# Two crossbar transposes of a tile each, joined into one transfer of two tiles, in a two-layer attention kernel

## The reference

```python
# first block                                   # second block
theta, phi = W_theta x + b, W_phi x + b         # h = group_norm(x1);  q, k, v = conv1x1(h)
f = softmax(theta^T phi / 8)                    # attn = softmax(q^T k * 128 ** -0.5)
x1 = x + W_fuse (f x) + b_fuse                  # y = x1 + W_p (attn v) + b_p
```

## Time and profile before

| | |
|---|---|
| median of 3 runs | 1957.88 us (1955.1 to 1966.29) |
| profiled execution | 1956.89 us, span 1955.1 us |
| PE busy | 1757.1 us, 90% |
| DVE busy | 1481.1 us, 76% |
| ACT busy | 1454.8 us, 74% |
| POOL busy | 1271.6 us, 65% |
| transposing transfers | 384, 4.5 us from issue to landing in the median |

### The profile page before, as it was taken

The page is one execution under the profiler, slowest core; times in us unless marked ns, Lnnn a source line. Parts: engine busy times, 40 slices in busy tenths (PEclk is TensorE's granted clock), DMA queues, the critical chain, the costliest instruction groups (busy, mean ns, idle before and its releaser), DMA issues.

```text
span 1955.1 us, 34447 instructions
## 1 busy us (share of the span) xinstructions
PE 1757.1 (90%) x8966; PEld 1202.4 (62%) x8966; DVE 1481.1 (76%) x1650; ACT 1454.8 (74%) x2152; POOL 1271.6 (65%) x1321
## 2 busy tenths in 40 slices
PE   5799999999999999999999999899999999989986
PEld 3566666666666666666666666666666666666654
DVE  4677777778777878777877777877777877787754
ACT  4577777777777777777777777777777777777764
POOL 2565776666776666776666776666676666776653
PEclk9899999999999999999999999999999999999999
DMA  3587787777777777787777778777778777767774
GB/s 76 113 152 140 150 160 153 148 153 149 150 160 153 152 146 149 149 162 154 145 152 149 151 160 157 143 149 149 152 152 162 145 149 150 151 148 155 144 133 92
DMA packets 860085, 286.33 MB, mean 146 GB/s; under 512 B 822304, under 2 KB 823200, under 8 KB 860064
## 3 DMA queue, kind: packets, MB, share of 16 engines
q1 hardware_dynamic: 860064, 286.08, 73.9%
HBM read 50.86 MB, written 17.04 MB: 35 GB/s over the span
## 4 chain that ended last, share of the span: by engine, by line
PE 47%; issue 22%; DVE 12%; POOL 9%; ACT 7%; DMA 1%; SPq 1%; DVEq 1%; POOLq 0%; ACTq 0%
PE o_ps L414 16%; PE s_ps L414 14%; PE m_ps L414 13%; PE s_ps L452 4%; ACT et L618 3%; POOL pair L837 2%; DVE phi L793 2%; DVE theta L789 2%; POOL y_sb L936 2%; DVE neg_max L700 2%; DVE x L754 2%; POOL h_lo L837 2%; ACT e_copied L608 2%; DVE den_scaled L729 1%; POOL rstd L877 1%
## 5 line engine op out<-in xcount | busy, mean ns | idle before, releaser
L414 PE MATMUL o_ps<-et,v_hi 128*128 128x512 f16 x2048 | 697.2, 382 | 89.0 <-DVE x L754 58.5
L700 DVE TENSOR_REDUCE neg_max<-s_ps 128x1 f32<-128x1024 f32 x512 | 625.6, 1222 | 127.1 <-PE s_ps L414 116.8
L414 PEld LDWEIGHTS o_ps<-et,v_hi 128*128 128x128 f16 x2048 | 202.4, 99 | 345.1 <-issue 163.6
L414 PE MATMUL o_ps<-et,v_lo 128*128 128x512 f16 x1024 | 389.5, 380 | 0.0
L608 ACT ACTIVATE s_ps<-s_ps,neg_max 128x1024 f32<-128x1024 f32 x256 | 278.3, 1087 | 111.4 <-DVE neg_max L700 110.5
L717 DVE SCALAR_TENSOR_TENSOR pair<-s_ps,pair 128x1024 f16<-128x1024 f32 x256 | 312.5, 1221 | 52.2 <-ACT pair L633 51.3
L414 PE MATMUL s_ps<-phi,theta 128*128 128x512 f32 x1024 | 331.9, 447 | 6.9 <-ACT e_copied L608 4.0
L711 DVE SCALAR_TENSOR_TENSOR et<-s_ps,et 128x1024 f16<-128x1024 f32 x128 | 156.7, 1225 | 219.7 <-ACT et L618 219.7
L837 POOL TENSOR_TENSOR pair<-e_copied,pair 128x1024 f16<-128x1024 f32 x128 | 274.3, 2143 | 16.5 <-ACT pair L631 16.5
L926 POOL TENSOR_TENSOR x<-x,xr 128x512 f32<-128x512 f32 x64 | 81.5, 1274 | 309.0 <-DVE x L754 309.0
L633 ACT ACTIVATE pair<-s_ps 128x1024 f16<-128x1024 f32 x256 | 261.9, 1023 | 8.1
(11 more groups left out here) (113 smaller groups left out, 3185.3 us busy)
## 6 DMA issues: line engine op xcount, KB each, us to landing
rden_row<-rden_dram SPq DMA_DIRECT2D x128, 256.0 KB, 3.8
xs<-in_x SPq DMA_DIRECT2D x32, 512.0 KB, 4.6
phi<-phi SPq DMA_DIRECT2D x64, 256.0 KB, 3.1
out_y<-y_sb SPq DMA_DIRECT2D x64, 256.0 KB, 2.7
et<-pair SPq DMA_TRANSPOSE x384, 4.5
rden_dram<-rden SPq DMA_DIRECT2D x128, 2.0 KB, 2.1
w_f<-in_w_fuse_t SPq DMA_DIRECT2D x1, 64.0 KB, 2.4
ident_sb<-in_ident SPq DMA_DIRECT2D x1, 64.0 KB, 2.2
```

The costliest lines, as they stand in the source:

```text
L414: mm = pe.matmul(out, lhs_t, rhs, start=start and n == 0, stop=stop and n == len(terms) - 1)
L700: nc.vector.tensor_reduce(neg_max[:, t % 4:t % 4 + 1], s_ps[:, part(t), :], AX.X, ALU.max, negate=True).then_inc(s_max, 1)
```

## The change

The second and third tile of a group share one transfer, of 2 x 2 x 1024 = 4096 numbers for each partition, issued where the third tile's was. The first tile keeps its own transfer. The three semaphores become two: one for the first tile, one for the other two. PE waits for two in quarter 0, and ACT waits for the second of them before it writes place 1 or place 2 of `pair`. In an iteration SP now issues T0 in slot 3, T1 with T2 in slot 4, T4 and then T5 with T6 in slot 8, T8 in slot 11, T9 with T10 in slot 12, T12 in slot 15, T13 with T14 in slot 0.

```diff
-        s_pair_t = [sem(f"pair_transposed{n}") for n in range(PAIRS)]
+        s_pair_t = [sem(n) for n in ("copied_transposed", "others_transposed")]
...
-                if here(crossed_at, it, s - 2):
+
+                if here(crossed_at, it, s - 2) and (s - 2) % GROUP == TURNED - 1:
                     move(it, s - 2, crossed_at, s_pair)
...
-                r = t % GROUP
                 sp.wait_ge(ready, before(kind, it, t) + 1)
...
-                sp.dma_start_transpose(et[:, t // GROUP % 4, r, :, :],
-                                       pair[:, r, :, :].rearrange("q a n -> q (a n)")).then_inc(s_pair_t[r], 16)
+                places = slice(COPIED, COPIED + 1) if kind is copied_at else slice(COPIED + 1, TURNED)
+                sp.dma_start_transpose(et[:, t // GROUP % 4, places, :, :].rearrange("k r b q -> k (r b) q"),
+                                       pair[:, places, :, :].rearrange("q r a n -> q (r a n)")
+                                       ).then_inc(s_pair_t[int(kind is crossed_at)], 16)
...
-                    for r in range(PAIRS):
+                    for r in range(2):
                         pe.wait_ge(s_pair_t[r], 16 * before(same_pair(r), it, first + GROUP))
...
-                act.wait_ge(s_pair_t[r], 16 * before(same_pair(t), it, t))
+                act.wait_ge(s_pair_t[min(r, 1)], 16 * before(same_pair(t), it, t))
```

## The result

The kernel with the joined transfers takes 2009.25 us in the median of 4 runs (2005.42 to 2018.24), against 1958.93 (1955.1 to 1966.29, 4 runs) for the one before: a ratio of 1.0259, 95% interval 1.0213 to 1.0305. It is slower, as forecast, but by 50 us instead of 20, and outside the range. The profiled execution took 2005.42 us with a span of 2003.6.

The account below looks back on a forecast made before the run. No engine is full; a chain through PE, issue, DVE, POOL and ACT bounds the kernel at 58.7 us an image. A loss of 0.67 us in 31 images, 20.8, on 1956.89 gives about 1978, range 1952 to 2002.

Parts of the forecast that it names:

- T5+T6 behind T4: Slot 8: the double lands at 812.5, 1.3 us too late for ACT's tile 9, making PE 0.82 us late an image.
- The other three places: Slots 4, 0 and 12, T1+T2, T13+T14 and T9+T10: a gain of 0.15 us an image, zero and zero.
- The rivals by which the change is faster or hidden: Second half about 1.4 us, time 1946, chance 0.08; or landing 0.4 earlier or delay absorbed, 1957 to 1966, chance 0.18.
- A double transfer that costs extra in itself: Rival: each double lands 0.5 us later than summed, striking slots 2, 6 and 10; 2024, or near 2180; chance 0.10.
- PE's wait for phi: Confirming sign before the unit at 815.69: PE's idle there grows from 0.51 to about 1.3 us.
- One sign that was to speak against the forecast: Slots 2 and 6 showing new waits on the transfer would prove the forecast wrong; no size given.
- It repeats closely, so I work in one image ... and multiply: Step taking the image around 774 to 833 us, 58.7 us long, as typical and multiplying its loss by 31.
- moves along: Slot 14: PE's 1.96 us wait for DVE's final product at 828.84 shifts with PE's delay and absorbs none of it.
- 0.82 - 0.15 + 0 = 0.67: Sum in us an image: loss at T5+T6, gain at T1+T2, zero at the other two groups; 20.8 over 31 images.
- The gain of 0.15: Slot 4: T1+T2 land at 797.2 against 797.4, shortening PE's 0.34 us wait before quarter 0 by 0.15 an image.

## Why the prediction was wrong

**Direction, place and mechanism: right, shown.** The loss is made by T5+T6 behind T4, through L633 of tile 9 (L635 after), DVE's low part and phi, to w1. T5+T6 were to land 7.1 after their issue, and did. The other three places were forecast to cost nothing, and with them alone joined the kernel is 0.45% faster. The rivals by which the change is faster or hidden needed a second half of less than 2.3 us; it measured 7.1 - 4.8 = 2.3. A double transfer that costs extra in itself is out too: T1+T2 and T13+T14 each landed 6.7 after issue. PE's wait for phi grew to 1.04 and not to 1.3, as PE had already waited 0.47 in slot 10. One sign that was to speak against the forecast did show in part: new waits on the transfer in slots 2 and 6. ACT has 15 of them, 9.2 us in all. The kernel with the other three groups joined has 15 such waits too, and is faster than before, so they carry little.

**The step that failed: "It repeats closely, so I work in one image ... and multiply".** The sum took an image of 58.7 us, a mean, and treated it as one kind; the prediction never mentioned the clock. The trace of before had more than one kind: 58.4, and 60.1 or more where TensorE's clock fell behind the idle stretch of slot 14, the very wait that stands in the earlier trace rows with 1.96. I took that wait only as something that "moves along". 15 of the 50 us are there, and without them the time, near 1994, would lie inside the range.

**"0.82 - 0.15 + 0 = 0.67": two terms mis-sized.** The first was 0.9. PE's w1 starts 837.86 - 824.72 = 13.14 after T4's issue, where it had started 815.69 - 803.48 = 12.21 after it: 0.93. T5+T6 went 0.1 later behind T4 than T6 had gone, and the rest is rounding at the hand-overs. The gain of 0.15 exists (58.3 against 58.4 with the other three joined), but must not be subtracted. T4's issue waits for POOL's low part, which did not come earlier when PE did: 26.5 us after the image's first evacuation in both kernels. ACT reached tile 9 sooner, and only waited longer there, 2.13 us and not 1.45. Of two waits in a row, the later one swallows what is gained before it, as long as its own source stands still.

**Small terms.** The ends of the span, before the first and behind the last evacuation, grew by 3 us; the forecast had nothing for them. In the image shown the queue held a double for 4.8 to 5.4 us, not 4.7; no wait comes of it that the lists show.

**Open.** Why 58.3 and 58.4 us an image meet few falls and 58.9 and 59.4 many, when the idle stretch is the same 1.96 us in each, no run here shows. That the length counts is shown for the two ways in which it was made longer; how it does is not, and it is not all: with the second tile late, but apart, there are 8 falls at the 58.4 us of before. One hint stands in the traces. In the kernel after, falls in slot 14 of neighbouring images are 61.4 us apart, in all ten such pairs, nearly the 61.0 that an image with a fall takes. In the kernel before, where an image with a fall mostly takes 60.1, none of the five has one in the next image.

## What to carry to other kernels

Joining transfers whose fixed part already overlaps saves little (here 0.15 to 0.2 us an image, where the last piece landed sooner), and it moves the landing of the first piece to that of the last. Before joining or reordering, write down for each piece who is next to write its source, and when, and do so for every transfer that changes its place in the queue. A second set of buffers made it harmless here. Where PE has a regular idle stretch, look at the granted clock behind it in every iteration, not in one; if it falls in some, a change of the iteration's length can change how many, and a comparison of two versions is fair only with the falls counted or taken away by a few spare products in the stretch.

## What the runs showed that was not expected

- Four products of 128x512 more for each image, read by nobody, make the kernel before 0.8% faster (1945.37 against 1959.17 us, ratio 0.9922): the work costs nothing in the idle stretch and keeps the clock up. With three of the four groups joined as well it is 1941.1 us, the lowest of all here, though these two intervals overlap.
- The same four products three slots earlier, on the path, make it 2.1% slower, 43 us, of which 0.9 us an image, 28 in all, is their own time; the rest comes with the clock, 23 falls against 5.
- 0.52 MB through the crossbar take 2.3 us when one transfer is behind another, and the same as the second half of a double transfer: 6.7 to 7.1 us to landing, in the image shown, against 4.3 to 4.5.
